# Rows of the last three sorted blocks by one-hot products from SBUF, for two of eight batches, between the layers

## What is computed

```python
x = x + L0_ffn(L0_cond(x, cond_8))      # top 2 of 8 experts per token, weights top_w
x = x + L1_ffn(L1_cond(x, cond_8))      # cond: silu(up) * gate, down; ffn: each expert its best 256 tokens
# L0_ffn, the part that matters here:
sel = take_along_axis(y, top_idx)       # the two expert results of each token
out = einsum('tkc,tk->tc', sel, top_w)  # their weighted sum
```

## Time and profile before

| | |
|---|---|
| time, median of 3 runs | 164.12 us (163.84 to 164.75) |
| profiled execution, first to last instruction (its span) | 150.0 us |
| device time around that span, by the median | 14.1 us |
| TensorE busy | 138.6 us, 92% |
| DVE, ACT, POOL busy | 94.5, 84.9, 61.4 us |
| mean granted TensorE clock | 0.991 |

### The profile page before, as it was taken

One profiled execution on the slowest core, in us unless ns is written; L12 is line 12 of the kernel. 1 busy time (PEld: TensorE's weight loads), 2 busy tenths in 40 slices (PEclk: granted clock), 3 DMA queues, 4 the chain that ended last, 5 costly groups with the idle time before them and its releaser, 6 DMA issues.

```text
span 150.0 us, 3681 instructions
## 1 busy us (share of the span) xinstructions
PE 138.6 (92%) x1139; PEld 122.1 (81%) x1139; DVE 94.5 (63%) x323; ACT 84.9 (57%) x259; POOL 61.4 (41%) x65
## 2 busy tenths in 40 slices
PE   7999887999999999999999997979998999999970
PEld 3765777999999999964789975748988999999960
DVE  5467947555556565452699777767242597748891
ACT  0688826777777666620377769985326255557400
POOL 5000376544477555560500000003677778777000
PEclk9999999999999999999999999999999999999996
DMA  4999614999999991113602940030022222457714
GB/s 142 357 403 315 216 37 89 312 367 393 394 396 342 300 331 37 38 36 88 211 0 116 400 190 0 0 153 2 19 56 50 56 50 59 152 174 236 254 47 140
DMA packets 12965, 26.10 MB, mean 174 GB/s; under 512 B 2082, under 2 KB 5538, under 8 KB 12562
## 3 DMA queue, kind: packets, MB, share of 16 engines
q1 hardware_dynamic: 10336, 21.54, 40.9%
q0 software_dynamic: 1760, 3.67, 8.1%
q10 hardware_dynamic: 850, 0.66, 1.3%
HBM read 19.92 MB, written 5.93 MB: 172 GB/s over the span
## 4 chain that ended last, share of the span: by engine, by line
PE 68%; DVE 14%; DMA 5%; issue 4%; ACT 3%; POOL 3%; DVEq 0%; ACTq 0%
PE bank L617 13%; PE bank L627 13%; PE bank L709 10%; PE bank L818 7%; PE bank L676 3%; PE bank L581 3%; DVE c_tok L1416 2%; POOL xg L476 2%; PE bank L685 2%; DMA got<-picked 2%; PE bank L508 2%; PE bank L770 2%; DMA xg<-rows,idx 2%; DMA picked<-y,sidx 1%; PE bank L543 1%
## 5 line engine op out<-in xcount | busy, mean ns | idle before, releaser
L952 ACT ACTIVATE hT<-bank,w_now 128x128 f32<-128x128 f32 x88 | 25.1, 368 | 11.5 <-PE bank L617 11.5
L1032 ACT ACTIVATE h1T<-bank,c_sb 128x256 f32<-128x256 f32 x44 | 18.3, 471 | 13.7 <-PE bank L709 13.7
L454 POOL DMA_INDIRECT xs<-rows,gidx x15 | 15.1, 1006 | 24.1 <-DVE gidx L1186 14.6
L627 PE MATMUL bank<-w_sb,hT 128*128 (+1 forms) x184 | 24.4, 276 | 0.3 <-ACT hT L952 0.3
L617 PE MATMUL bank<-xg,w_now 128*128 (+1 forms) x176 | 23.4, 276 | 0.8 <-ACT xg L936 0.8
L627 PEld LDWEIGHTS bank<-w_sb,hT 128*128 128x128 f32 x184 | 22.4, 192 | 0.5 <-ACT hT L952 0.5
L617 PEld LDWEIGHTS bank<-xg,w_now 128*128 128x128 f32 x176 | 21.4, 192 | 1.1 <-issue 1.0
L459 POOL DMA_INDIRECT picked<-y,sidx x16 | 15.7, 979 | 10.0 <-DVE y L1233 8.5
L476 POOL DMA_INDIRECT xg<-rows,idx x14 | 14.8, 1054 | 5.0 <-issue 3.7
L1233 DVE SCALAR_TENSOR_TENSOR y<-bank,pairm,y 128x128 f32 (+1 forms) x23 | 8.1, 351 | 10.2 <-PE bank L627 10.0
L709 PE MATMUL bank<-xgT,v_sb 128*128 128x256 f32 x56 | 14.2, 384 | 0.0
(11 more groups left out here) (214 smaller groups left out, 246.9 us busy)
## 6 DMA issues: line engine op xcount, KB each, us to landing
v_sb<-in_v SPq DMA_DIRECT2D x16, 256.0 KB
cw_sb<-in_cond_w SPq DMA_DIRECT2D x8, 386.5 KB
plane<-y SPq DMA_DIRECT2D x5, 512.0 KB, 5.1
w_sb<-plane SPq DMA_DIRECT2D x10, 256.0 KB, 3.1
w_sb<-in_w SPq DMA_DIRECT2D x2, 1024.0 KB, 7.6
w_sb<-in_w SPq DMA_DIRECT2D x1, 1290.0 KB, 7.9
w_sb<-in_w SPq DMA_DIRECT2D x1, 774.0 KB, 5.8
rows<-row SPq DMA_DIRECT2D x1, 544.0 KB, 3.3
```

The costliest lines, as they stand in the source:

```text
L454: pool.indirect_dma_start(out=xs[:, b % RING], out_offset=None, in_=rows0, in_offset=rows_at(gidx, b)).then_inc(gathered[b % RING], 16)
L627: mm = pe.matmul(bank[6 + j % 2][:, 0:C], hT[:, j % 2, P * f:P * f + P], w2_sb[:, bass.ds(e * (NF * C) + f * C, C)], start=(f == 0), stop= ...
L952: ins = act.activation(hT[:, j % 2, P * f:P * f + P], bank[2 + j % 2][:, P * f:P * f + P], ACT.Relu, bias=w1_of[:, F + f:F + f + 1])
L1032: act.activation(h1T[:, n % 2, fc], bank[UP_BANKS[(2 * n + h) % 4]][:, CAP * f:CAP * f + CAP], ACT.Gelu, bias=c1_sb[:, e * NF + fc:e * NF ...
```

## The change

Blocks 13, 14 and 15 are called late (`LATE = 3`), batches 0 and 1 early (`EARLY = 2`). SP reads `picked` for the early batches as soon as the first 13 scatters have landed. Rows of late blocks that belong to early batches are scattered to a spare half of `picked` (`late_idx`), and their places in the first half are cleared to zero at the start by two DMAs. Instead, TensorE adds them into the two transposed sums by products of `y0[:, 13 + i]` with `late_1h`, a matrix of 128 x 256 that DVE makes: at (row, token) the row's gate where the row's token is this one, else 0. For that each row's gate must be known by row: SP stores `wt` to a DRAM tensor `gates`, and POOL gathers it by three indirect DMAs, placed behind gather(11), (13) and (15). The softmax weights and `gate_diag` are computed within DVE's pair loop. Batches 0 and 1 go through layer 1's FFN first, their `x1` is won back by two transpositions and a copy (`turn_back`), and ACT's DMA issues for the other batches stand between silu(0) and silu(1). The `keep_warm` of 24 goes.

```diff
-        picked = nc.dram_tensor("picked", (K * T, C), F32).ap()
+        picked = nc.dram_tensor("picked", (2 * K * T, C), F32).ap()
+        gates = nc.dram_tensor("gates", (K * T, 1), F32).ap()
...
-        PIECES = [(0, 1), (1, 2), (2, 4), (4, NC)]
+        PIECES = [(EARLY, 4), (4, NC)]
...   (SP)
+            sp.wait_ge(y0_cleared, 2)
+            for k in range(K):
+                load(picked_of(k, 0, EARLY), no_rows, picked_cleared)
             sp.wait_ge(x_turned, 3)
             load(w2_sb[:, W2H:], w2[:, W2H:], in_w2_late)
...
                 load(v2_sb[:, e].rearrange("p f c -> p (f c)"), v2[:, e * NF * C:(e + 1) * NF * C], in_v)
+                if e == 2:
+                    sp.wait_ge(wt_ready, 1)
+                    load(gates.rearrange("(k p c) o -> p k (c o)", k=K, p=P), wt[:], gates_written)
...
-            sp.wait_ge(scattered, NB * 16)
+            sp.wait_ge(scattered, FIRST_LATE * 16)
+            for k in range(K):
+                load(got[:, k, 0:EARLY], picked_of(k, 0, EARLY), early_in)
+            sp.wait_ge(scattered_late, LATE * 16)
             for h, (c0, c1_) in enumerate(PIECES):
                 load(got[:, 0, c0:c1_], picked_of(0, c0, c1_), got_in[h])
...   (POOL)
+            def gather_gate(i):
+                pool.wait_ge(gates_written, 16)
+                pool.indirect_dma_start(out=late_gate[:, i:i + 1], out_offset=None, in_=gates,
+                                        in_offset=rows_at(sidx, FIRST_LATE + i)).then_inc(late_gates_in, 16)
+
             for b in range(1, NB):
                 gather(b)
+                if b in (11, 13, 15):
+                    gather_gate((b - 11) // 2)
...   (TensorE)
-            keep_warm(bank[4], 24)
+            def late_rows(b, i):
+                pe.wait_ge(y_kept, min(FIRST_LATE + i + E, NPAIR))
+                return pe.matmul(bank[b][:, 0:P], y0[:, FIRST_LATE + i], late_1h[:, i, P * b:P * b + P],
+                                 start=False, stop=(i == LATE - 1))
...
+            sum_early(0)
+            sum_early(1)
+            up_gate(0)
+            up_gate(1)
+            turn_back()
+            down1(0)
+            down1(1)
+            turn_d(0)
+            turn_d(1)
+            for b in range(EARLY, NC + 3):
...   (ACT)
+            take_x1(0)
+            take_x1(1)
+            silu(0)
+            act.wait_ge(scattered_late, LATE * 16)
+            for h, (c0, c1_) in enumerate(PIECES):
+                act.dma_start(got[:, 1, c0:c1_], picked_of(1, c0, c1_)).then_inc(got_in[h], 16)
+            silu(1)
+            act.wait_ge(x1_back, 1)
+            act.activation(x1[:, 0:EARLY].rearrange("p c d -> p (c d)"), bank[6][:, 0:EARLY * P], ACT.Copy).then_inc(x1_copied, 1)
+            take_d(0)
+            take_d(1)
+            squash(0)
+            take_row(0)
+            squash(1)
+            take_row(1)
...   (DVE)
+            def gates_and_late(j):
...
+                if j == 3:
+                    v.tensor_tensor(wt[:, 1], wt[:, 0], den[:], ALU.mult).then_inc(wt_ready, 1)
...
+                if NPAIR - 4 <= j < NPAIR - 4 + LATE:
+                    i = j - (NPAIR - 4)
+                    ins = v.tensor_scalar(late_1h[:, i], token_key[:], late_token[:, i:i + 1], late_gate[:, i:i + 1],
+                                          ALU.is_equal, ALU.mult)
...
                 bias(j)
+                gates_and_late(j)
                 keep(j)
...
-            for b in range(NC):
-                for c in {0: (2,), 1: (3,), 2: (4, 5), 3: (6, 7)}.get(b, ()):
+            for b in range(EARLY, NC):
+                for c in {2: (4, 5), 3: (6,), 4: (7,)}.get(b, ()):
```

More of the change, by code:

```diff
@@ L215, in adaln_moe @@
         got = sb("got", [P, K, NC, C])
-        TURNED_SUMS = 2
-        gate_diag = sb("gate_diag", [P, TURNED_SUMS, K, P])
+        EARLY = 2
+        LATE = 3
+        FIRST_LATE = NB - LATE
+        gate_diag = sb("gate_diag", [P, EARLY, K, P])
+        late_gate = sb("late_gate", [P, LATE])
+        late_token = sb("late_token", [P, LATE])
+        late_batch = sb("late_batch", [P, LATE], I32)
+        late_shift = sb("late_shift", [P, LATE], I32)
+        late_idx = sb("late_idx", [P, LATE], I32)
+        token_key = sb("token_key", [P, EARLY * P], I16)
+        late_1h = sb("late_1h", [P, LATE, EARLY * P])
         xa = bsc[:].rearrange("p (c d) -> p c d", c=NC)
+        no_rows = y0[:, 2 * NC:2 * NC + EARLY]
         cols0 = w2_sb[:, 3 * T:4 * T].bitcast(BF16).rearrange("p (s i) -> p s i", i=K * NC)
@@ L366, in picked_of @@
         def picked_of(k, c0, c1_):
-            return picked.rearrange("(k p c) d -> k p c d", k=K, c=NC)[k, :, c0:c1_]
+            return picked[0:K * T].rearrange("(k p c) d -> k p c d", k=K, c=NC)[k, :, c0:c1_]
         def plane_of(e, g):
@@ L651, in _, with sum_early, turn_back @@
                     down0(j - 2)
+            def late_rows(b, i):
+                pe.wait_ge(y_kept, min(FIRST_LATE + i + E, NPAIR))
+                return pe.matmul(bank[b][:, 0:P], y0[:, FIRST_LATE + i], late_1h[:, i, P * b:P * b + P],
+                                 start=False, stop=(i == LATE - 1))
             pe.wait_ge(in_x, 16)
-            for b in range(TURNED_SUMS):
+            pe.wait_ge(late_1h_ready, 1)
+            for b in range(EARLY):
                 pe.matmul(bank[b][:, 0:P], x_sb[:, b], ident, start=True, stop=False)
-            keep_warm(bank[4], 24)
+                for i in range(LATE - 1):
+                    late_rows(b, i)
             pe.wait_ge(in_cw, 16 * NC)
-            def turn_x1(b):
[L660 to L668, removed]
+            def sum_early(b):
+                pe.wait_ge(gate_diag_ready, 1)
+                pe.wait_ge(early_in, 32)
+                for k in range(K):
+                    pe.matmul(bank[b][:, 0:P], got[:, k, b], gate_diag[:, b, k], start=False, stop=False)
+                late_rows(b, LATE - 1).then_inc(x1_turned, 1)
+            def turn_back():
+                for b in range(EARLY):
+                    mm = pe.transpose(bank[6][:, P * b:P * b + P], x1T[:, b], ident)
+                mm.then_inc(x1_back, 1)
+            def turn_x1(b):
+                pe.wait_ge(x1_ready, b + 1 - EARLY)
+                pe.wait_ge(x1T_ready, b - 1 if b == EARLY else b)
                 pe.transpose(bank[0][:, 0:P], x1[:, b], ident).then_inc(x1_turned, 1)
@@ L715, in _ @@
             pe.wait_ge(in_v, 16 * 2 * E)
-            for b in range(NC + 3):
-                if b < NC and b != TURNED_SUMS:
+            sum_early(0)
[8 more added lines that the diff above has]
+            for b in range(EARLY, NC + 3):
+                if b < NC:
                     turn_x1(b)
-                if 0 <= b - 1 < NC:
+                if EARLY <= b - 1 < NC:
                     up_gate(b - 1)
-                if b == TURNED_SUMS:
-                    turn_x1(b)
                 if b > NC:
                     up1(0, 0, (b - NC - 1,))
-                if 0 <= b - 3 < NC:
+                if EARLY <= b - 3:
                     turn_d(b - 3)
-                if 0 <= b - 2 < NC:
+                if EARLY <= b - 2 < NC:
                     down1(b - 2)
@@ L1234, in keep @@
                                        ALU.add).then_inc(y_kept, 1)
+            def gates_and_late(j):
+                if j == 1:
+                    v.wait_ge(exp_ready, 2)
+                    link(v.tensor_reduce(zsum[:], expd[:], AX.X, ALU.add))
+                    link(v.scalar_tensor_tensor(den2[:], zsum[:], 1e-9, den[:], ALU.mult, ALU.add))
+                if j == 2:
+                    link(v.tensor_scalar(den2[:], den2[:], 1.0, None, ALU.add))
+                    link(v.reciprocal(wt[:, 0], den2[:]))
+                if j == 3:
+                    v.tensor_tensor(wt[:, 1], wt[:, 0], den[:], ALU.mult).then_inc(wt_ready, 1)
+                    v.wait_ge(wt_ready, 1)
+                if j == 4:
+                    late = sidx[:, FIRST_LATE:NB]
+                    v.tensor_copy(late_token[:], gidx[:, FIRST_LATE:NB])
+                    link(v.tensor_scalar(late_batch[:], late, NC - 1, None, ALU.bitwise_and))
+                    link(v.tensor_scalar(late_shift[:], late_batch[:], float(EARLY), float(K * T), ALU.is_lt, ALU.mult))
+                if j == 5:
+                    v.tensor_tensor(late_idx[:], sidx[:, FIRST_LATE:NB], late_shift[:], ALU.add).then_inc(late_idx_ready, 1)
+                if j in (6, 7):
+                    for k in range(K):
+                        ins = v.tensor_scalar(gate_diag[:, j - 6, k], ident_sb[:], wt[:, k, j - 6:j - 5], None, ALU.mult)
+                    if j == 7:
+                        ins.then_inc(gate_diag_ready, 1)
+                if j == NPAIR - 4:
+                    v.wait_ge(late_gates_in, 16 * LATE)
+                    v.wait_ge(y0_cleared, 3)
+                if NPAIR - 4 <= j < NPAIR - 4 + LATE:
+                    i = j - (NPAIR - 4)
```

(13 more changed lines are left out.)

45 lines of the change are left out of this document (29 added, 16 removed).

## The result

The changed kernel takes 170.35 us (median of 4), the kernel before 163.98 in the same comparison: a ratio of 1.045 (1.038 to 1.052), slower, where 168.8 was forecast. The mechanism of the forecast is in the trace.

A forecast was written before the change was run, and what follows sets the result against it. TensorE's L617 and L627 in turn, fed by POOL's gathers, were taken to bound the pair loop; stall 4.3 plus clock 1.4 less seam gain 1.0 made +4.7 on 164.1, so 168.8 us, range 164.3 to 171.5.

The forecast's parts named there:

- The gates land at 39.5: SP's store of the gates waits behind 3,720 KB of loads on its queue, landing at 39.5 (bounds 37.9 and 41.0).
- The stall: 4.3: Pair loop: gather(12) waits on POOL behind the first gate gather, so TensorE stalls 4.3 us before turn_x(12); bounds 2.1, 6.6.
- The clock: 1.4: Behind the pair loop's stall TensorE runs at half rate for about 2.7 us, costing 1.4 us; bounds 0 and 2.7.
- the first rival: TensorE's clock holds through the pair loop's stall, a stall near 2.1 being too short: 167.4 us; chance 25%.
- DVE's work and the cleared rows: 0: DVE's added pair-loop work hides in idle time and slack, clearing picked is free: cost 0, at worst 0.3 us.
- The seam: 1.0: Between the layers, up_gate(2) starts at about 75.1 against 76.17: gain 1.0 us, bounds 0.5 and 1.5.
- The sum: Whole kernel: 4.3 + 1.4 - 1.0 = +4.7 us on 164.1, giving 168.8 us.
- the gates weren't in time: Denies the rival that the gates' store lands by 36, nearly without stall, making the change faster: 163.1 us; chance 12%.
- the third rival: Between the layers nothing is gained: early reads land later or ACT's chain is longer, up_gate(2) starts as before; 169.8 us, 8%.

The follow-up runs named there:

- the gathers last: Changed kernel with the three gate gathers moved behind gather(15) on POOL: ratio to the kernel before 0.999, on another occasion 1.000.
- experiment 5: Changed kernel with the gates' store issued by ACT, not SP: 157.22 us, ratio 1.031 to before; also stored as 128 rows, landing in 5.9 us.
- the round trip alone: Kernel before plus only the gates' store, the three gate gathers at 11, 13, 15 and softmax weights in the pair loop: 159.83 us, ratio 1.045.
- experiment 7: Changed kernel, unchanged, timed again beside the kernel before: 167.64 us against 162.83 (ratio 1.040), then 158.8 against 153.16 (1.028).
- experiment 8: Changed kernel with gate gathers behind gather(15), plus batch 2's reads and turn_x1(2) moved earlier: 151.42 us, ratio 0.987 to the kernel before.
- experiment 6: Changed kernel with the first gate gather behind gather(14), the other two behind gather(15): 166.57 us, ratio 1.017 to the kernel before.
- experiment 4: 17 idle products before turn_x(12): in the changed kernel 169.24 us, ratio 1.049; in the kernel before with only the gates' round trip, 1.034.

## Why the forecast held, point by point

The mechanism was right: the wait on POOL, the late gather(12), TensorE's stall, the clock, the seam's small gain. The sizes agree in part by luck, as the points say, and one reason behind them was wrong.

- **The gates land at 39.5.** They landed at 40.82 (33.51 + 7.31) in the changed kernel and at 39.7 with the gathers last. The size was near, the reason wrong: "it stands in SP's queue behind" 3.7 MB isn't what holds it, since on ACT's queue it takes 7.1 us, with nothing ahead. The ring order that the Trainium skill states ("DMA: Bandwidth & Descriptors", queues, rings and completion order) isn't refuted by that, only not what decides here. The Trainium skill also says ("DMA: Bandwidth & Descriptors", issuing engines are not separate DMA queues) that DMAs run on the same 16 engines whichever engine issues them; 7.1 us on one queue and 7.3 to 8.4 on the other agree with that. The b2 load of the earlier trace rows had misled me: it is 512 KB, no small transfer, and went out while the engines were full. The right number came from a wrong sum.
- **The stall: 4.3.** Measured 4.1 to 4.7 in the six traces with the store on SP's queue. In the first of them (4.2) the parts were off and cancelled: gather(12) went out 1.6 us later than forecast, landed in 4.5 instead of 6.0, TensorE took it up 1.1 us after it had landed, and turn_x(12)'s own place was 1.3 us later (43.75 instead of 42.46). The quick landing goes with engines that run empty once TensorE's stall holds back the paced loads (389 GB/s at 44 to 46, 95 at 46 to 48); in the two traces without unexplained pauses it was 5.1. (The chain of the earlier trace rows has 42 groups of eight, not 43, with a turn between them up to turn_x(15); nothing hangs on it.)
- **The clock: 1.4.** It fell, as forecast, and even in the stall of 2.4 us of experiment 5, where the first rival had called 2.1 too short. Its price was 1.6, 1.9 and 2.8 us in three traces, so this term was too small, at worst just above its upper bound of 2.7. The forecast let TensorE run at half rate for 2.7 us; it did for 3.0 in the round trip alone (47.7 to 50.7) and for 5.5 in experiment 7 (47.5 to 53.0). Holding the clock by idle products gave some 1.7 back.
- **DVE's work and the cleared rows: 0.** From turn_x(12) to the last keep it takes 23.6 us with the gathers last as in the kernel before, in two traces of each. Right.
- **The seam: 1.0.** up_gate(2) starts 8.6 to 9.4 us after the last keep in the nine traces with this seam (9.1 in the first), and 9.7 to 10.1 in the four with the old one; the means are 9.0 and 9.9. By DVE's first sum of the threshold search (`coarse_sum`), which follows the last batch's scores, it is 22.9 to 23.7 against 24.4 to 24.8, 1.3 us between the means. So the seam gives the forecast microsecond. Yet the time is that of before (1.000). It is given back in layer 1's tail: from that sum to the end of the span 59.1 and 59.7 us in two profiles of before, 60.0 and 61.0 with the gathers last. There the third turn of gathered rows comes 25.7 to 25.9 us after the sum instead of 25.1 to 25.2, behind xg gathers that land later; why they do, and what the rest is, stays open. ACT's issues in front of silu(1) cost less than I reckoned (they were issued under silu(0)); the early reads landed 0.7 us later than forecast in one trace and in time in the other. That batches 0 and 1 run alone, and that this eats most of their gain, is supported by experiment 8.
- **The sum.** 4.3 + 1.4 - 1.0 = 4.7 on 164.1. The measured differences of the medians were 6.4 and 4.8 us where before takes 164 and 162.8, and 5.6 where it takes 153 (4.3 by the ratio). They lie around 4.7, but they aren't made of its three terms alone: in the traced execution of experiment 7, 6.7 us over before, stall and clock make 7.4. The base of 164.1 was itself a time with pauses that no term of the sum knew, and in the first trace one of them lies under the stall and others at the pair loop and at 122 to 130, where the clock falls again. How much of the first difference goes with them isn't shown, for no trace of before exists in such surroundings; which instruction supply, queue or neighbour causes them, no run here settles. That 170.35 came within 1.6 us of 168.8 is therefore luck in part.
- **The rivals.** The clock didn't hold, and the gates weren't in time. The seam's gain is nil by the end of the kernel, as the third rival had it, but not in its way: up_gate(2) does start sooner.

## What to carry to other kernels

A wait put into an in-order queue that also feeds the bound engine is priced by what stands behind it, not by itself: three gathers moved behind the last one it feeds took the whole loss away. A small transfer while the DMA engines are full is not quick on an empty queue either (7.1 us here, 7.3 to 8.4 behind loads), so read the landing times of the transfers beside it (5.4 to 6.8) before reckoning with 2 or 3 us. Work that starts earlier is worth only what the next work to be let in can follow: here letting batch 2 in sooner brought 1.3%, where starting two batches some four microseconds sooner alone had brought nothing.

## What the runs showed of the hardware

- The kernel before took 152 to 153 us on two occasions and 163 to 164 on two others. The five traces taken on the latter, all of changed kernels, have pauses of 3 to 6 us that nothing of the kernel ends, such as ACT's here in the run of experiment 6, which held TensorE for 4.90 us:

```profile
52.74 1.14 ACT L1017 ACTIVATE hT<-bank,w_now 128x128 f32<-128x128 f32 x4 [5.41 <-remote]
...
54.02 1.80 PE L671 MATMUL bank<-w_sb,hT 128*128 x8 [4.90 <-ACT hT L1017]
```

- A store of 8 KB took 7.3 to 8.4 us to land on SP's queue and 7.1 on ACT's, while the engines moved some 370 to 410 GB/s, and 5.9 with half as many rows (one landing).
- TensorE's clock fell to its lower level in every unfilled stall of 2.4 to 4.6 us in front of turn_x(12), at a price of 1.6 to 2.8 us where no unexplained pause lay behind it; with 3.83 us of products in a stall of 4.7 us it held.
- In one execution TensorE's products took twice their time from 7 to 16 us while the profile gave the granted clock as 1.00 (experiment 4).
